# A mixture of experts behind a decoder: rooms of the small experts cut from 128 slots down to 90

## The chip, the core and the metric
The kernel runs on one core of a Trainium2 chip, as one program. The metric is the device time of one execution in microseconds. The kernel before took 1332.15 us, the median of three runs between 1330.96 and 1334.1 us.

## The reference, cut to what matters
```python
x = x + attn(layernorm(x), ...)                 # a state-space scan, 16 x 256 x 256
x = x + align(ctx_1024, layernorm(x))           # dynamic time warping against the context
x = x + ffn(layernorm(x), gate, w0, w1, wo)     # 64 experts, each token goes to 2 of them

# ffn, x is now 4096 tokens x 256
gate_logits = x @ gate                          # 4096 x 64
weights, selected = top_k(gate_logits, 2)
weights = softmax(weights)
# tokens sorted by expert, group_sizes[e] of them for expert e:
h0 = ragged_dot(sorted_x, w0, group_sizes)      # w0, w1: 64 x 256 x 512
h1 = ragged_dot(sorted_x, w1, group_sizes)
out_sorted = ragged_dot(silu(h0) * h1, wo, group_sizes)   # wo: 64 x 512 x 256
out = sum over the 2 experts of weights * unsorted(out_sorted)
```
All of it is float32. The 8192 places (4096 tokens, two experts each) fall on 64 experts, 128 each in the mean. How many each expert gets is known only on the chip.

## The kernel before, in words
The program has five stages, one after the other: `states` (the scan and the distances), `wave` and `trace_back` (the alignment), `expand` (the aligned rows are added, tokens are normalised, routed and listed by expert) and `experts`. The change touches only constants that `expand` and `experts` are built from.

**Rooms.** The experts are ranked by the number of their tokens, most first. The rank fixes how many slots an expert's turn has, its room. `ROOMS` (L47) is a list of entries (first rank, number of ranks, ranks per step, first width, step), and `ROOM` (L48) spreads it out to 64 widths. Ranks 0 to 31 are wide (129 to 256 slots, two tiles of tokens), ranks 32 to 63 narrow (128 at most, one tile). Before, the wide rooms fall from 220 to 134 and the narrow ones are all 128. An expert with more tokens than its room gets late turns for the rest. `LATE` (L56) is the largest possible number of them, and `K.late_n`, which the chip computes, the true number plus one: the last rank, 63, has no turn of its own but always takes the first late turn.

**Order of turns.** `TURN` (L152) alternates: rank 0, 32, 1, 33, ... 31. So 63 turns k are written out, wide for even k and narrow for odd k, and then comes a loop over late turns that runs `late_n` times.

**One turn** (TensorE, L2309 to L2328). With n = room:
- `turn` (L2259, record L2265) transposes the gathered tokens of the next turn into `mo_xt_ps`.
- `up` (L2272, L2279), for each of four blocks m of 128 of the 512 hidden units: four float32 matmuls, stationary operand a 128x128 block of `w0` or `w1`, moving operand n columns of tokens. The profile has two records for one float32 matmul, so 32 records a turn.
- ScalarE makes SiLU of one half of `mo_h` (L2361), VectorE multiplies by the other half (L2408) into `mo_inter`.
- narrow turns: `down` (L2283, L2285), stationary `mo_inter` of n columns, moving 256 columns of `wo`, 8 records. Wide turns: `down_wide` (L2288, L2293), stationary `wo`, moving n columns, 16 records; ScalarE copies the result (L2371) and `back` (L2298, L2304) transposes it inside the next turn.
- VectorE copies the result to `mo_o` (L2419).

The order on TensorE is up 0, up 1, (back of the turn before, if that was wide), up 2, down 0, up 3, down 1, turn of the next, down 2, down 3.

**Queues.** GpSimd gathers tokens four turns ahead by indirect DMA (`gather`, L2213, one for each tile of up to 128 rows) and scatters results (`scatter`, L2220), in the order gather(k+4), scatter(k). Only n rows are moved. SyncE loads the 1.5 MB of weights of turn k once turn k-4 has done its down matmuls (`load_weights`, L2119; ring of four). After the last turn SyncE reads all results back, and VectorE adds them to x with their weights (L2482).

**Constants.** In `expand`, GpSimd writes the rooms into `ro_room` with one IOTA for each entry of `ROOMS` (L1662), then about thirty other constants, between the masks of batch 1 and those of batch 2 (L1645), which TensorE needs for the sums of that batch (L2029). The gate's logits are the matmul at L2050: stationary 128x128 tokens, moving 64 columns of the gate. Tables of late turns (`ro_place`, `ro_at`, `late_of`, `late_at`) have `LATE` or `LATE + 2` columns.

Of the kernel before, what the change touches and what calls it, by code (L numbers as in the profile page):

```python
# [43 lines left out]
WRING = 4  # L44
RANKS = E - 1
WIDE = E // 2
ROOMS = ((0, 2, 1, 220, 20), (2, 14, 2, 190, 6), (16, 16, 2, 148, 2), (32, 32, 32, 128, 0))  # L47
ROOM = [top - step * (i // run) for _, n, run, top, step in ROOMS for i in range(n)]  # L48


# [1472 lines left out]
def expand(K):  # L1523
# [5 lines left out]
    with ExitStack() as c:  # L1529
# [89 lines left out]
        tile = lambda t: K.x[:, t, :]  # L1619
        ALL = 31 + len(ROOMS) + 1  # L1620
        real = lambda b: 0 <= b < B
# [14 lines left out]
        def _(pool):  # L1636
# [23 lines left out]
            def routing_constants():  # L1660
                for r, n, run_, first, step in ROOMS:
                    nc.gpsimd.iota(room[:, r:r + n].rearrange("p (i a) -> p i a", a=run_),  # L1662
# [6 lines left out]
                               ).then_inc(constant, 1)  # L1669
                pool.wait_ge(constant, len(ROOMS) + 4)  # L1670
                nc.gpsimd.affine_select(out=before[:, :], in_=before[:, :], compare_op=ALU.is_gt, fill=0.0,
# [921 lines left out]
```

## Time and profile before
| | us |
|---|---|
| median of three runs | 1332.15 |
| the profiled execution | 1334.92 |
| its span, first to last instruction | 1333.2 |
| TensorE busy | 1051.0 (79%) |
| VectorE busy | 922.2 (69%) |
| ScalarE busy | 577.5 (43%) |
| GpSimd busy | 637.2 (48%) |
| `mo_h` matmuls, 2048 records | 284.2, 290 ns mean |
| SiLU, 256 ACTIVATEs | 71.6, 290 ns mean |

The granted clock of TensorE is 0.886 in the mean. The experts' loop lies between about 835 and 1296 us of the span. A record's duration in this table is its latency; matmuls overlap, so what one costs in a stream is the distance between starts. There are 256 SiLUs, four for each of 64 turns: 63 written out and one late turn.

### The profile page before, as it was taken

Reading aid. Unit: us, or ns where it says so; the run is one execution under the profiler, and the core shown is the slowest. Engines: PE = TensorE matmul, PEld = TensorE weight load, DVE = VectorE, ACT = ScalarE, POOL = GpSimd, SP = SyncE. Lnnn points to the kernel's source line nnn. Section 1 sums busy time; section 2 is a strip of 40 time slices with the busy share of each in tenths; the row PEclk is TensorE's granted clock in tenths of the full one; section 3 lists DMA queues with packets and bytes.
Section 4 is the critical chain, followed back from the end, with each engine's and each line's share of the span. In section 5 each row is a group of like instructions: output and inputs, shape, how many; then the busy total and the mean of one; then the engine's idle time right before and its main releaser. Section 6 shows DMA issues by size and latency. Waiting matters only on the chain. (4 is left out here: it accounts for less than half of the span.)

```text
span 1333.2 us, 21073 instructions
## 1 busy us (share of the span) xinstructions
PE 1051.0 (79%) x6867; PEld 931.6 (70%) x6867; DVE 922.2 (69%) x2071; ACT 577.5 (43%) x1286; POOL 637.2 (48%) x609
## 2 busy tenths in 40 slices
PE   5767878787887875777826886999999999989970
PEld 4656767677776765666412775899999888888860
DVE  6999999999999993888786897233332333222348
ACT  3768787877778672443601652212212111111110
POOL 4886978888786960200003552344344443433420
PEclk8899899999999898555767996899999999999985
DMA  8544546464646532022130112888788788877729
GB/s 241 188 141 140 172 139 198 137 192 151 188 160 187 168 105 66 17 48 32 32 125 2 56 49 76 289 270 274 260 269 279 259 270 274 266 262 262 253 94 352
DMA packets 161165, 231.41 MB, mean 174 GB/s; under 512 B 32157, under 2 KB 85773, under 8 KB 160417
## 3 DMA queue, kind: packets, MB, share of 16 engines
q1 hardware_dynamic: 145520, 206.67, 49.2%
q0 software_dynamic: 9200, 18.96, 4.1%
q10 hardware_dynamic: 6336, 4.44, 1.0%
q8 instruction: 55, 0.90, 0.3%
q14 instruction: 54, 0.43, 0.1%
HBM read 203.01 MB, written 22.80 MB: 169 GB/s over the span
## 5 line engine op out<-in xcount | busy, mean ns | idle before, releaser
L1010 PE MATMUL st_y_ps<-ident,st_hc 128*128 128x128 f32 x2048 | 274.8, 292 | 110.8 <-DVE st_hc L529 110.8
L1010 PEld LDWEIGHTS st_y_ps<-ident,st_hc 128*128 128x128 f32 x2048 | 256.8, 204 | 132.9 <-DVE st_hc L529 132.1
L412 POOL TENSOR_TENSOR st_u<-st_dx,codes 128x1024 f32<-128x1024 f32 x127 | 296.4, 2359 | 39.3 <-DVE st_h L521 31.5
L521 DVE TENSOR_TENSOR_SCAN st_h<-st_da,st_u 128x512 f32<-128x512 f32 x256 | 297.6, 1203 | 0.2 <-POOL st_u L412 0.2
L2279 PE MATMUL mo_h<-mo_xt,w 128*128 128x128 f32 (+17 forms) x2048 | 284.2, 290 | 2.0 <-DVE mo_xt L2402 2.0
L2279 PEld LDWEIGHTS mo_h<-mo_xt,w 128*128 128x128 f32 x2048 | 273.7, 194 | 6.7 <-issue 2.7
L2408 DVE TENSOR_TENSOR mo_inter<-mo_silu,mo_h 128x128 f32<-128x128 f32 (+17 forms) x256 | 75.5, 303 | 280.2 <-ACT mo_silu L2361 217.6
L2361 ACT ACTIVATE mo_silu<-mo_h 128x128 f32<-128x128 f32 (+17 forms) x256 | 71.6, 290 | 315.5 <-PE mo_h L2279 224.9
L2220 POOL DMA_INDIRECT outs<-mo_o,choice x95 | 93.7, 986 | 234.8 <-DVE mo_o L2419 221.0
L748 ACT ACTIVATE st_da<-st_delta,st_a_neg 128x510 f32<-128x510 f32 x256 | 172.1, 685 | 58.3 <-DVE st_h L521 53.7
L529 DVE TENSOR_TENSOR st_hc<-st_h,st_cps 128x1024 f32<-128x1024 f32 x128 | 152.5, 1192 | 0.0
L1294 PE MATMUL wv_e<-wv_r,wv_shift 128*128 128x1 f32 x274 | 75.9, 347 | 40.4 <-DVE wv_r L1232 39.5
L2213 POOL DMA_INDIRECT mo_xg<-xn,table x93 | 90.6, 975 | 33.6 <-issue 28.1
L2293 PE MATMUL mo_ot_ps<-mo_inter,wo 128*128 128x190 f32 (+16 forms) x512 | 89.8, 309 | 17.5 <-DVE mo_inter L2408 14.2
L1294 PEld LDWEIGHTS wv_e<-wv_r,wv_shift 128*128 128x128 f32 x274 | 68.5, 312 | 48.1 <-issue 46.1
L755 ACT ACTIVATE st_cps<-codes 128x512 f32<-128x512 f32 x128 | 76.7, 599 | 43.3 <-DVE st_hc L529 42.2
L2293 PEld LDWEIGHTS mo_ot_ps<-mo_inter,wo 128*128 128x128 f32 x512 | 74.3, 192 | 25.3 <-DVE mo_inter L2408 19.8
L1645 POOL TENSOR_SCALAR ex_on<-ex_apart,ex_reach 128x256 f32<-128x256 f32 x32 | 30.4, 961 | 95.0 <-ACT ex_apart L1972 94.9
L2285 PE MATMUL mo_o_ps<-wo,mo_inter 128*128 128x256 f32 x256 | 73.9, 392 | 0.0
L1284 ACT ACTIVATE wv_r<-wv_e,wv_edge_big 128x1 f32<-128x1 f32 x137 | 35.8, 261 | 64.6 <-PE wv_e L1294 64.6
L1232 DVE TENSOR_TENSOR_SCAN wv_r<-wv_m,wv_r,wave 128x64 f32<-128x64 f32 x136 | 47.8, 352 | 4.8
L2419 DVE COPY mo_o<-mo_o_ps 128x256 f32<-128x256 f32 (+16 forms) x95 | 36.8, 415 | 19.7 <-PE mo_o_ps L2285 17.2
(393 smaller groups left out, 1437.5 us busy)
## 6 DMA issues: line engine op xcount, KB each, us to landing
codes<-bc SPq DMA_DIRECT2D x256, 256.0 KB, 3.7
w<-in_L_ffn_w_dram SPq DMA_DIRECT2D x128, 512.0 KB
wo<-in_L_ffn_wo_dram SPq DMA_DIRECT2D x64, 512.0 KB
co_got<-outs SPq DMA_DIRECT2D x16, 512.0 KB, 6.1
wave<-dist SPq DMA_DIRECT2D x16, 274.0 KB
x<-in_x_dram SPq DMA_DIRECT2D x8, 512.0 KB, 9.1
st_cx<-in_ctx_dram SPq DMA_DIRECT2D x8, 512.0 KB, 4.0
dist<-st_dd SPq DMA_DIRECT2D x32, 128.0 KB, 3.4
```

The costliest lines, as they stand in the source:

```text
L412: nc.gpsimd.tensor_tensor(u_sb[k % URING][:, :, :], dx[p % 2][:, :, :], over_chunks(b_sb[k % BRING]), ALU.mult).then_inc(u_ok, 1)
L521: nc.vector.tensor_tensor_scan(h_sb[k % HRING][:, dh, :], da_ps[dh][:, :], u_sb[k % URING][:, dh, :], 0.0, ALU.mult, ALU.add).then_inc(h_o ...
L529: nc.vector.tensor_tensor(hc_sb[k % RING][:, :, :], h_sb[k % HRING][:, :, :], over_chunks(c_ps[k % 2][:, :]), ALU.mult).then_inc(hc_ok, 1)
L748: nc.scalar.activation(by_batch(da_ps[dh][:, :]), by_batch(delta[p % 2][:, dh, :]), ACT.Exp, scale=a_neg[:, dh, n:n + 1]).then_inc(da_ok, 1)
L755: nc.scalar.activation(c_ps[k % 2][:, :], c_sb[k % CRING], ACT.Copy).then_inc(c_ok, 1)
L1010: m = nc.tensor.matmul(y_ps[t // 2][:, t % 2, dh * P:(dh + 1) * P], hc_sb[k % RING][:, dh, t * P:(t + 1) * P], K.ident[:, :], start=False, ...
L1294: nc.tensor.matmul(e_ps[t % 4][:, 0:1], K.shift[:, :], r[:, t + 1, SW:SW + 1], start=True, stop=True).then_inc(e_mm, 1)
L2213: nc.gpsimd.indirect_dma_start(xg[k % XR][0:n, a, :], None, K.xn_dram[:, :], bass.IndirectOffsetOnAxis(ap=K.table[0:n, at:at + 1], axis=0) ...
L2220: nc.gpsimd.indirect_dma_start(K.outs_dram[:, :], bass.IndirectOffsetOnAxis(ap=K.choice[0:n, at:at + 1], axis=0), o_sb[k % XR][0:n, a, :], ...
L2279: ins = nc.tensor.matmul(h_ps[m][:, i, 0:n], K.w[r][i][:, c_, m * P:(m + 1) * P], xt[u][:, c_, 0:n], start=(c_ == 0), stop=(c_ == DC - 1))
L2293: ins = nc.tensor.matmul(ot_ps[:, c_, 0:n], K.w[r][2][:, m, c_ * P:(c_ + 1) * P], inter[m][:, 0:n], start=(m == 0 and c_ == 0), stop=(m == ...
L2408: nc.vector.tensor_tensor(inter[m][:, 0:n], silu[m][:, 0:n], h_ps[m][:, 1, 0:n], ALU.mult).then_inc(inter_ok, 1)
```

## The change
```diff
-ROOMS = ((0, 2, 1, 220, 20), (2, 14, 2, 190, 6), (16, 16, 2, 148, 2), (32, 32, 32, 128, 0))
+ROOMS = ((0, 2, 1, 220, 20), (2, 14, 2, 190, 6), (16, 16, 2, 148, 2), (32, 8, 8, 128, 0), (40, 16, 1, 124, 1),
+         (56, 7, 1, 108, 3), (63, 1, 1, 128, 0))
```
Ranks 32 to 39 keep 128 slots. Ranks 40 to 55 get 124, 123, ... 109, ranks 56 to 62 get 108, 105, ... 90, and rank 63 keeps 128. Every operation whose size is `room[k]` follows in the turns k = 17, 19, ... 61: the moving columns of `up` and `turn`, the stationary columns of `down`, SiLU and product, the rows of gather, scatter and of the copy to `mo_o`. `LATE` becomes 66 instead of 64, and three more IOTA fill `ro_room`. Nothing else changes, neither the order of turns nor a wait.

## Rows read from the trace of the kernel before
**Rows 1.** By stretch: PE, PEld, DVE, ACT, POOL busy, clock, DMA share, GB/s
```profile
860.00:900.00 40.00, 40.00 (x276) 38.47 (x275) 12.96 (x37) 8.00 (x25) 15.97 (x17) 1.00 0.80 267
...
1140.00:1180.00 40.00, 36.46 (x266) 34.08 (x266) 12.15 (x38) 7.03 (x25) 14.49 (x15) 0.96 0.77 258
```
**Rows 2.** Chain of waits, experts' loop: start, us, what
```profile
1053.55 3.14 PE mo_h L2279 x24
...
1061.11 1.78 PE mo_h L2279 x16
```
**Rows 3.** Waits of SyncE's queue: total us, times, longest
```profile
SPq L156 <- PE mo_ot_ps L2293: 145.0, 29, 6.8
```
**Rows 4.** Timeline, a narrow turn on TensorE: start, us, engine, line, operation, shape, count
```profile
1228.13 1.95 PE L2279 MATMUL mo_h<-mo_xt,w 128*128 128x128 f32 x16
1229.91 0.60 PE L2304 MATMUL mo_o_ps<-ident,mo_ot 128*128 128x128 f32 x4
...
1234.50 2.94 PE L2279 MATMUL mo_h<-mo_xt,w 128*128 128x136 f32 x24
```
**Rows 5.** Timeline, wide turns of 184 and of 136 columns
```profile
912.44 3.90 PE L2279 MATMUL mo_h<-mo_xt,w 128*128 128x184 f32 x24
916.18 0.79 PE L2293 MATMUL mo_ot_ps<-mo_inter,wo 128*128 128x184 f32 x4
...
1237.28 0.63 PE L2293 MATMUL mo_ot_ps<-mo_inter,wo 128*128 128x136 f32 x4
...
1240.17 0.46 ACT L2361 ACTIVATE mo_silu<-mo_h 128x136 f32<-128x136 f32 x2 [2.58 <-PE mo_h L2279]
...
1240.84 1.19 PE L2293 MATMUL mo_ot_ps<-mo_inter,wo 128*128 128x136 f32 x8 [1.32 <-DVE mo_inter L2408]
1241.87 1.39 PE L2279 MATMUL mo_h<-mo_xt,w 128*128 128x128 f32 x11
```
**Rows 6.** Timeline, routing stage, a matmul of 64 moving columns
```profile
752.58 1.06 PE L2050 MATMUL ex_l<-gate,ex_xt 128*128 128x64 f32 x8
753.47 1.08 PE L2029 MATMUL ex_e<-codes,ex_on 128*128 128x256 f32 x4
```
**Rows 7.** Timeline, GpSimd's scatters: 8 rows of a second tile, then 128 rows
```profile
1232.98 0.88 POOL L2220 DMA_INDIRECT outs<-mo_o,choice  x1 [0.30 <-issue]
...
1235.47 1.00 POOL L2220 DMA_INDIRECT outs<-mo_o,choice  x1 [0.30 <-DVE mo_o L2419]
```
**Rows 8.** Timeline, constants, the mask behind them, and who waits for it
```profile
725.85 0.59 POOL L1662 IOTA ro_room<- 128x2 f32 x4
...
731.68 1.82 POOL L1645 TENSOR_SCALAR ex_on<-ex_apart,ex_reach 128x256 f32<-128x256 f32 x2
...
733.56 1.13 PE L2029 MATMUL ex_e<-codes,ex_on 128*128 128x256 f32 x4 [1.34 <-POOL ex_on L1645]
```
**Rows 9.** Timeline, openings, scatters and SiLUs of two wide turns that differ
```profile
1038.77 3.30 PE L2279 MATMUL mo_h<-mo_xt,w 128*128 128x154 f32 x24
1039.71 1.00 POOL L2220 DMA_INDIRECT outs<-mo_o,choice  x1 [0.30 <-DVE mo_o L2419]
...
1044.40 0.68 ACT L2361 ACTIVATE mo_silu<-mo_h 128x154 f32<-128x154 f32 x3 [3.96 <-PE mo_h L2279]
...
1047.00 1.95 PE L2279 MATMUL mo_h<-mo_xt,w 128*128 128x128 f32 x16
...
1095.10 3.14 PE L2279 MATMUL mo_h<-mo_xt,w 128*128 128x146 f32 x24
1097.41 0.99 POOL L2220 DMA_INDIRECT outs<-mo_o,choice  x1 [1.63 <-issue]
...
1101.29 1.95 PE L2279 MATMUL mo_h<-mo_xt,w 128*128 128x128 f32 x16
```
**Rows 10.** Timeline, the late turn: its transposes, and the next gather's landing
```profile
1281.48 0.43 PE L2265 MATMUL mo_xt_ps<-ident,mo_xg 128*128 128x128 f32 x2 [0.52 <-issue]
...
1303.05 0.50 POOL L2250 COPY mo_to<-mo_to_next 128x1 int32<-128x1 int32 x1 [5.60 <-DMA mo_xg<-xn,mo_index]
```

## The prediction
> **What bounds the kernel now.** I read the engines' shares stage by stage first. From 860 to 900 us TensorE is busy for all 40 of 40 us, from 1140 to 1180 for 36.5, at a granted clock of 1.00 (2.4 GHz) and 0.96, while the DMA engines are busy 77 to 80% of the time, VectorE 30% and ScalarE 20% or less [rows 1]. This is the loop over the experts, the only stage in which the width of a room is a loop size. The chain of waits for it has TensorE in nearly every link: turns of a wide and of a narrow expert alternate, and 16 records of `mo_h` in 1.78 us open each narrow turn [rows 2]. SyncE, which fetches the weights, waits 145.0 us for the wide turns alone to free a buffer [rows 3]: weights are not late on average. So what TensorE does in a narrow turn sets the price of a narrower room, and nothing hides a gain there: one narrow turn runs from 1228.13 to 1234.50, 6.37 us, and its records have no idle before them [rows 4].
>
> **The change, part by part.** By the new list ranks 40 to 55 lose 4, 5, ... 19 slots (184 together), ranks 56 to 62 lose 20, 23, ... 38 (203): 387 slots in 23 narrow turns, 16.8 each. The last expert keeps 128.
>
> (a) *The up matmuls*, 32 records a turn, move n columns past 128x128 weights. A record's price is the distance between starts: at 128 columns 16 records in 1229.91 - 1228.13 = 1.78 us, 111.3 ns each [rows 4]. At 184 columns 24 records take 916.18 - 912.44 = 3.74 us, 155.8 ns; at 136 columns 1237.28 - 1234.50 = 2.78 us, 115.8 ns [rows 4, 5]. That is 0.833 ns per column, and carried on it would give 109.2 ns at 128; the measured 111.3 is already above the line. The deciding row is the gate matmul of the routing stage, of the same type and with a 128x128 stationary operand too, but with 64 columns: 8 records from 752.58 to 753.47, again 111.3 ns [rows 6]. Half the columns, the same pace. Every record has a load of 128 columns of weights in front, whatever the room, and I take that as what sets the pace below about 130 columns. Bounds: nothing (the 64-column row), or the column rate carried down, 387 columns x 32 records x 0.833 ns = 10.3 us; a loss has no ground, since fewer columns can't take TensorE longer. The widths in question, 90 to 124, lie between 64 and 128, where both ends cost the same, so I take 0.
>
> The Trainium skill gives two readings of this, both in TensorE: Matmul & The Clock Gate. Its section on the back-to-back issue gap has a formula linear in the moving columns; its section on LDWEIGHTS charges a load by its columns alone, some 107 ns for 128. By the first the edit would gain about 10 us, by the second nothing. The 64-column row agrees with the second.
>
> (b) *The down matmuls* of a narrow expert hold the activations as stationary operand, now of n columns, and move 256 columns of `wo`. At 0.833 ns per column those 256 take 213 ns a record, more than a load, and they stay. Only the first load at a joint could show: if loads shrink with their columns, 16.8/128 x 111.3 = 15 ns, at three joints a turn 23 x 3 x 15 = 1.0 us at most, 0 at least. I take 0, because TensorE has no idle at those joints now [rows 4].
>
> (c) *Turning the tokens in* (two records in the wide turn ahead) moves n columns past 128 columns of stationary operand: same floor as (a), 0. *SiLU and product*: two SiLUs of 136 columns take 0.46 us [rows 5]; even if each shrank by 13%, 0.03 us, TensorE's stream hides it in narrow turns: 0. With that cover gone it would be 4 x 0.03 x 23 = 2.8 us.
>
> (d) *Gather and scatter* carry 387 rows less each way. GpSimd issues a scatter of 128 rows in 1.00 us and that of the 8 rows of a second tile in 0.88 [rows 7]: 1 ns per row, 0.02 us per issue, on an engine that is busy 16 of 40 us [rows 1]. The bytes, 0.8 MB at about 260 GB/s, are 3 us of DMA time spread over 300 us in which DMA is 80% busy [rows 1]. Directly 0, at most 3 us; what a shift of phase does is a rival.
>
> (e) *Setting up.* The list of rooms has 7 entries instead of 4, so GpSimd issues three more IOTA into `ro_room`. Four take 0.59 us, 0.15 each. GpSimd goes from these constants to the mask of the third batch with no idle, and TensorE waits 1.34 us for that mask [rows 8]. So +0.4 us stands on the path; 0 is the lower end, if later beats, in which GpSimd waits for ScalarE, take it back. `LATE` grows from 64 to 66, which lengthens a handful of small VectorE operations by two columns: 0.
>
> (f) *Overflow.* An expert with more tokens than its room gets a late turn more. I worked the counts out of the reference's own inputs. Sorted they are 206, 188, ..., and from rank 40 on 114 (room 124), ..., 96 (99), 95 (96), 91 (93), 74 (90), 51 (128). None is over, so the loop of late turns still runs once, but the closest margin is one token.
>
> **The sum**: 0 (a) + 0 (b to d) + 0.4 (e) + 0 (f) = +0.4 us, which takes the profiled execution from 1334.92 to 1335.3 us. That execution lies 2.8 us above the median of the runs, 1332.15, so I forecast **1332.5 us**, with a range of its own from 1329.6 to 1334.8. A change under 0.2%, 2.7 us, can't be told from none in this kernel.
>
> **The rivals.**
>
> *Late SiLUs in wide turns, for the better.* The 50 records of a wide turn of 136 columns should take some 5.9 us at 0.116 each; the turn takes 1241.87 - 1234.50 = 7.37 us [rows 4, 5]. ScalarE is late in it: its third and fourth SiLU start at 1240.17, although the 24 records that hold the third group of up matmuls end by 1237.44, and then TensorE idles 1.32 us for the product [rows 5]. I can't name what holds ScalarE; DMA issues by SyncE and GpSimd fall in the same stretch. In one turn of 146 columns GpSimd's scatter came 1097.41 - 1095.10 = 2.3 us after the opening and not 1.0, and the turn took 1101.29 - 1095.10 = 6.19 us [rows 9]. If fewer rows relieve whatever it is, a cured turn gives 1.3 us: five give 6.5 us, all 23 give 30. Against it: the rooms shorten an issue by 0.02 us only. Near 1326 us, chance 0.18.
>
> *The same, for the worse (slower than before).* The place is GpSimd's scatter of the narrow tile, in the wide turn behind it. It now starts 0.97 us after the opening (1235.47 against 1234.50) [rows 4, 7]. In an earlier turn it started after 0.94 us (1039.71 against 1038.77), three of four SiLUs came only at 1044.40, and the turn took 1047.00 - 1038.77 = 8.23 us, where the next one of equal width took 1061.11 - 1053.55 = 7.56 by the chain [rows 2, 9]. A shorter gather in front pulls the scatter forward by 0.02 us, to just there. Each turn that tips costs 0.67 us; five decide, since they make 3 us, and 23 would cost 15. Against it: it is one example. About 1337 us, chance 0.15.
>
> *The columns do pay.* The floor in (a) is not there and the up matmuls follow the column rate: 1332.5 - 10.3 = 1322.2 us. For it speaks the straight line through 184 and 136 columns, against it the 64-column row. Chance 0.06.
>
> *It doesn't do what it says.* If the chip's routing differs from my counts by a token or two, the smaller room overflows and adds a late turn. The present one lasts from its transposes at 1281.48 to the landing of the next gather, 1303.05, 21.6 us [rows 10]: 1354 us for one. Chance 0.03.
>
> **How the numbers follow.** The forecast has 0.58, the rivals 0.18, 0.15, 0.06 and 0.03. Faster is 0.18 + 0.06 = 0.24, slower 0.15 + 0.03 = 0.18, within 0.2% 0.58. The range leaves out the column rate, the overflow and the far ends of both SiLU cases, about 2 in 10 with the tails: 1325 to 1338 us.
>
> **What would show it.** Right: openings of narrow turns still take 1.78 us for 16 records, at 90 columns too, and narrow turns stay at 6.37 us; seven IOTA in `ro_room` and TensorE's wait for the third mask some 0.4 us longer; 256 SiLUs as before. Wrong: openings that shrink with the room (16 records of 90 columns near 1.27 us by the column rate); wide turns away from 7.4 us on either side; more than 256 SiLUs; a granted clock clearly under that of before in the second half of the loop.

## The result and the profile after

The changed kernel takes 1322.82 us (median of four runs, 1321.91 to 1323.03) against 1333.12 us (1330.96 to 1335.77) for the kernel before beside it: a ratio of 0.9928, 95% interval 0.9913 to 0.9942. That is 10.3 us or 0.7% faster, 9.7 us below the forecast of 1332.5 us and outside its range. The profiled executions are 1334.92 and 1322.75 us, 12.2 apart. About 2 of these are a single wide turn of the execution before, which took 9.47 us where its neighbours of the same width took 7.46.

From the page of the changed kernel: GpSimd's DMA queue (packets, MB, share of 16 engines) and the groups of the up matmuls, the scatters and the gathers.

```profile
q0 software_dynamic: 13456, 18.23, 4.3%
...
L2280 PE MATMUL mo_h<-mo_xt,w 128*128 128x128 f32 (+40 forms) x2048 | 279.8, 288 | 2.0 <-DVE mo_xt L2403 2.0
...
L2221 POOL DMA_INDIRECT outs<-mo_o,choice x95 | 100.1, 1054 | 208.9 <-DVE mo_o L2420 185.5
...
L2214 POOL DMA_INDIRECT mo_xg<-xn,table x93 | 97.5, 1049 | 33.7 <-issue 28.1
```

The up matmuls, the place where the rooms are a loop size, went from 284.2 to 279.8 us of busy time, and as will be seen that is nearly all overlap. Scatters and gathers, which carry fewer rows now, became longer: their means were 986 and 975 ns before and are 1054 and 1049 ns. The queue has 13,456 packets for 18.23 MB, where it had 9,200 for 18.96 MB.

I cut the span at two events: the first up matmul of turn 0, and the transposes that open the late turn. Before they stand at 836.89 us and 1281.48 [rows 10], after at 839.02 and 1270.98. So the written-out turns take 432.0 us and not 444.6, which is 12.6 less; the start is 2.1 later, and what follows the loop 1.7 shorter (50.0 against 51.7). Read link by link in the chain of waits, the 12.6 are 10.6 from the 23 wide turns of ranks 8 to 30, 1.5 from all narrow turns, and the rest from the first wide ones. Of the 10.6, five wide turns described below give 6.3, the turn of 9.47 us gives 1.9, and the others together 2.4. **The change is made to narrow turns, and the gain lies in wide ones.**

**Narrow turns.** Timeline of TensorE, the last narrow turn, room 90:

```profile
1257.38 1.92 PE L2280 MATMUL mo_h<-mo_xt,w 128*128 128x90 f32 x16
1259.14 0.60 PE L2305 MATMUL mo_o_ps<-ident,mo_ot 128*128 128x128 f32 x4
...
1263.62 2.56 PE L2280 MATMUL mo_h<-mo_xt,w 128*128 128x134 f32 x21
```

The opening of 16 records lasts 1259.14 - 1257.38 = 1.76 us, where 128 columns took 1.78 [rows 4]; the column rate asked for 1.27. The turn takes 6.24 us and not 6.37.

**Wide turns.** Two wide turns of nearly one width. First the turn that opens at 1171.16, with the scatter of a tile of 109 rows (the DVE copy `mo_o` shows the rows):

```profile
1171.16 3.02 PE L2280 MATMUL mo_h<-mo_xt,w 128*128 128x140 f32 x24
1171.37 0.42 DVE L2420 COPY mo_o<-mo_o_ps 109x256 f32<-109x256 f32 x1 [0.60 <-issue]
1172.14 2.34 POOL L2221 DMA_INDIRECT outs<-mo_o,choice  x1 [0.30 <-DVE mo_o L2420]
1172.32 0.29 ACT L2362 ACTIVATE mo_silu<-mo_h 128x140 f32<-128x140 f32 x1 [2.61 <-PE mo_h L2280]
...
1174.06 0.47 ACT L2362 ACTIVATE mo_silu<-mo_h 128x140 f32<-128x140 f32 x2 [1.46 <-PE mo_h L2280]
...
1174.79 0.99 POOL L2214 DMA_INDIRECT mo_xg<-xn,table  x1 [0.31 <-issue]
...
1175.65 0.29 ACT L2362 ACTIVATE mo_silu<-mo_h 128x140 f32<-128x140 f32 x1 [1.13 <-issue]
...
1177.09 1.93 PE L2280 MATMUL mo_h<-mo_xt,w 128*128 128x108 f32 x16
```

Then the one that opens at 1157.36, with a tile of 110 rows:

```profile
1157.36 3.06 PE L2280 MATMUL mo_h<-mo_xt,w 128*128 128x142 f32 x24
1157.56 0.42 DVE L2420 COPY mo_o<-mo_o_ps 110x256 f32<-110x256 f32 x1 [0.59 <-PE mo_o_ps L2286]
1158.37 1.01 POOL L2221 DMA_INDIRECT outs<-mo_o,choice  x1 [0.30 <-issue]
...
1159.69 0.99 POOL L2214 DMA_INDIRECT mo_xg<-xn,table  x1 [0.30 <-issue]
...
...
1161.62 0.29 ACT L2362 ACTIVATE mo_silu<-mo_h 128x142 f32<-128x142 f32 x1 [2.81 <-PE mo_h L2280]
...
1163.11 0.47 ACT L2362 ACTIVATE mo_silu<-mo_h 128x142 f32<-128x142 f32 x2 [1.19 <-PE mo_h L2280]
...
1163.79 1.23 PE L2294 MATMUL mo_ot_ps<-mo_inter,wo 128*128 128x142 f32 x8 [0.54 <-DVE mo_inter L2409]
...
1164.86 1.37 PE L2280 MATMUL mo_h<-mo_xt,w 128*128 128x109 f32 x11
```

The first takes 1177.09 - 1171.16 = 5.93 us, its last SiLU starts 4.5 us after the opening, and no wait is written at its matmuls. The second takes 7.50 us as turns did before, the last two SiLUs start 5.75 us after the opening and right behind that, and TensorE idles. What differs on GpSimd is one number: the scatter of 109 rows holds it for 2.34 us, that of 110 rows for 1.01, so the gathers of the wide tile start 3.63 us after the opening and not 2.33. The 23 wide turns are of these two kinds and some between. One turn each of 144, 142 and 140 columns takes 6.09, 6.01 and 5.93 us, one of 154 takes 6.49 and one of 160 6.74, where all took 7.4 to 7.6 before. These five are turns with a long issue: the tile of 113 rows has its scatter in the first of them, that of 109 rows its gather in the second (2.36 us) and its scatter in the third, the tile of 118 rows its scatter (1.67 us) in that of 154 columns and its gather (1.68 us) in that of 160. A turn of 146 columns takes 6.17 us, but one of that width took 6.19 before too [rows 9]. The other turns from 146 columns down keep 7.1 to 7.5, one takes 8.15, and the last, of 134 columns, takes 5.67 where it took 5.70.

**Setting up.** Timeline of the constants of `expand`:

```profile
725.72 1.03 POOL L1663 IOTA ro_room<- 128x2 f32 x7
...
733.87 1.19 PE L2030 MATMUL ex_e<-codes,ex_on 128*128 128x256 f32 x4 [2.47 <-POOL ex_on L1646]
```

### The profile page after: what moved, and what is told of

It is laid out like the page before. It is cut to its first block and busy times, and to the rows that moved or that the text cites. A ratio compares the mean times of both kernels' runs of the same rounds, so it can differ in the third digit from the quotient of the medians.

```text
span 1321.0 us, 21076 instructions
## 1 busy us (share of the span) xinstructions
PE 1039.5 (79%) x6867; PEld 921.1 (70%) x6867; DVE 921.6 (70%) x2071; ACT 577.0 (44%) x1286; POOL 650.8 (49%) x612
## 3 DMA queue, kind: packets, MB, share of 16 engines
q0 software_dynamic: 13456, 18.23, 4.3%
## 5 line engine op out<-in xcount | busy, mean ns | idle before, releaser
L2280 PE MATMUL mo_h<-mo_xt,w 128*128 128x128 f32 (+40 forms) x2048 | 279.8, 288 | 2.0 <-DVE mo_xt L2403 2.0
L2280 PEld LDWEIGHTS mo_h<-mo_xt,w 128*128 128x128 f32 x2048 | 270.2, 192 | 7.3 <-issue 2.7
L2409 DVE TENSOR_TENSOR mo_inter<-mo_silu,mo_h 128x128 f32<-128x128 f32 (+35 forms) x256 | 74.9, 297 | 267.7 <-ACT mo_silu L2362 213.1
L2362 ACT ACTIVATE mo_silu<-mo_h 128x128 f32<-128x128 f32 (+35 forms) x256 | 71.5, 286 | 303.9 <-PE mo_h L2280 209.8
L2221 POOL DMA_INDIRECT outs<-mo_o,choice x95 | 100.1, 1054 | 208.9 <-DVE mo_o L2420 185.5
L749 ACT ACTIVATE st_da<-st_delta,st_a_neg 128x510 f32<-128x510 f32 x256 | 172.1, 685 | 58.4 <-DVE st_h L522 54.0
L2214 POOL DMA_INDIRECT mo_xg<-xn,table x93 | 97.5, 1049 | 33.7 <-issue 28.1
L2294 PEld LDWEIGHTS mo_ot_ps<-mo_inter,wo 128*128 128x128 f32 x512 | 73.6, 190 | 16.3 <-DVE mo_inter L2409 12.2
L2286 PE MATMUL mo_o_ps<-wo,mo_inter 128*128 128x256 f32 (+23 forms) x256 | 74.1, 392 | 0.9 <-DVE mo_inter L2409 0.9
```

The costliest lines, as they stand in the source:

```text
L749: nc.scalar.activation(by_batch(da_ps[dh][:, :]), by_batch(delta[p % 2][:, dh, :]), ACT.Exp, scale=a_neg[:, dh, n:n + 1]).then_inc(da_ok, 1)
L2214: nc.gpsimd.indirect_dma_start(xg[k % XR][0:n, a, :], None, K.xn_dram[:, :], bass.IndirectOffsetOnAxis(ap=K.table[0:n, at:at + 1], axis=0) ...
L2221: nc.gpsimd.indirect_dma_start(K.outs_dram[:, :], bass.IndirectOffsetOnAxis(ap=K.choice[0:n, at:at + 1], axis=0), o_sb[k % XR][0:n, a, :], ...
L2280: ins = nc.tensor.matmul(h_ps[m][:, i, 0:n], K.w[r][i][:, c_, m * P:(m + 1) * P], xt[u][:, c_, 0:n], start=(c_ == 0), stop=(c_ == DC - 1))
L2286: nc.tensor.matmul(o_ps[k % 2 if isinstance(k, int) else RANKS % 2][0:n, 0, :], inter[m][:, 0:n], K.w[r][2][:, m, :], start=(m == 0), stop ...
L2294: ins = nc.tensor.matmul(ot_ps[:, c_, 0:n], K.w[r][2][:, m, c_ * P:(c_ + 1) * P], inter[m][:, 0:n], start=(m == 0 and c_ == 0), stop=(m == ...
```

## The experiments

They ran in three groups, each beside its own runs of the kernel before (medians 1346.33, 1331.69 and 1331.57 us). The first of these is 1.1% above the others, so each kernel is compared inside its group. All are edits of the kernel before unless said.

### 1. Which half of the change: rows or columns

`e1_rows_only` moves the rows of the changed kernel and computes on the old rooms:

```diff
+MOVES = (... (32, 8, 8, 128, 0), (40, 16, 1, 124, 1), (56, 7, 1, 108, 3), (63, 1, 1, 128, 0))
+rows = lambda k: [(a, at, min(n, MOVED[TURN[k]] - a * P)) for a, at, n in tiles_of(k)]
-                for a, at, n in tiles(k):
+                for a, at, n in rows(k):
```

> The rooms of before (128 columns in every narrow turn), but the gathers and scatters of the 23 narrow experts carry only as many rows as in the changed kernel (124 ... 90). Theory A (row counts): the 10 us come from GpSimd, whose indirect DMAs last 1.0 us for 128 rows but 1.3 to 2.4 us for 123, 122, 118, 113, 109 rows and so on, and so push GpSimd's later issues in a wide turn out of the stretch in which SyncE issues weights; then this kernel is 8 to 12 us faster than before, 1321 to 1325 us, with narrow turns at 6.37 us and wide turns between 5.9 and 7.5 us. Rival B (columns): the matmuls, SiLUs and products of fewer columns bring the time; then it is within 2 us of before.

`e2_columns_only` is the changed kernel, but its narrow gathers and scatters carry 128 rows:

```diff
+rows = lambda k: tiles_of(k) if TURN[k] < WIDE else [(a, at, P) for a, at, _ in tiles_of(k)]
```

> The rooms of the changed kernel for everything computed, but gathers and scatters of narrow experts carry 128 rows again (the surplus goes to dump rows). Theory A: the gain goes; 1331 to 1333 us, wide turns at 7.4 to 7.5 us again, narrow turns 6.24 to 6.37 us, which is 1 to 2 us in all. Rival B: it stays at 1322 to 1324 us.

`e3_rooms_of_16` has rooms that are multiples of 16, with 336 slots less:

```diff
-ROOMS = (... (32, 32, 32, 128, 0))
+ROOMS = (... (32, 14, 14, 128, 0), (46, 13, 13, 112, 0), (59, 4, 4, 96, 0), (63, 1, 1, 128, 0))
```

> Rooms that are multiples of 16: ranks 32 to 45 have 128, 46 to 58 have 112, 59 to 62 have 96; 336 slots fewer than before where the changed kernel has 387 fewer. Theory A: an indirect DMA of 112 or 96 rows lasts 0.94 to 1.0 us, so GpSimd's issues don't move; 1330.5 to 1333.5 us. Rival B (columns or bytes): 336/387 of the gain, some 1324 us.

The times expected were for a kernel before of 1332 us, and this group lies 14 us higher. Measured in it: rows alone 1329.55 us, ratio 0.9875 (0.9849 to 0.99); columns alone 1346.4, 1.0002 (0.9987 to 1.0018); rooms of 16 1344.68, 0.9991 (0.9977 to 1.0005). The whole gain is in the rows of the DMAs; beside its own kernel before `e1` gains 16.8 us, more than the 8 to 12 expected. The third says that it is not the number of rows either: 336 fewer bring nothing, 387 fewer bring 1.2%. Which counts do? Rows of the changed kernel's timeline, copies of a result tile and the scatters of that tile:

```profile
998.18 0.42 DVE L2420 COPY mo_o<-mo_o_ps 122x256 f32<-122x256 f32 x1 [0.55 <-PE mo_o_ps L2286]
999.16 1.68 POOL L2221 DMA_INDIRECT outs<-mo_o,choice  x1 [0.31 <-issue]
```

```profile
1118.36 0.42 DVE L2420 COPY mo_o<-mo_o_ps 113x256 f32<-113x256 f32 x1 [0.59 <-PE mo_o_ps L2286]
...
1119.52 2.38 POOL L2221 DMA_INDIRECT outs<-mo_o,choice  x1 [0.30 <-issue]
...
1130.77 0.42 DVE L2420 COPY mo_o<-mo_o_ps 112x256 f32<-112x256 f32 x1 [0.59 <-PE mo_o_ps L2286]
1131.57 0.96 POOL L2221 DMA_INDIRECT outs<-mo_o,choice  x1 [0.30 <-issue]
```

113 rows take 2.38 us, 112 take 0.96, 122 take 1.68. The other counts fall in place by the largest divisor up to 16. No such divisor but 1 (109, 113): 2.34 and 2.38 us. 2 (118, 122): 1.67, 1.68. 3 (93, 111, 123): 1.33 to 1.42. 4 (116, 124): 1.29, 1.35. 5 to 7 (115, 114, 102, 119): 1.10 to 1.17. From 11 on (99, 110, 121, 108, 117, 90, 105, 120, 96, 112 and 128): 0.94 to 1.04. With s the rows for each share, it is about 0.88 + 0.0133 s us, from 128 rows in 16 shares (s = 8, 1.00) to 113 in one (2.38); an estimate from these rows, and 61 rows in a share give 1.69 by it, measured 1.68.

The Trainium skill has the rule behind this pattern, in DMA: Bandwidth & Descriptors, section "Why a DMA increments its semaphore by 16 and not by 1": a transfer is spread over k engines, k being the largest number up to 16 that divides its slowest dimension. This trace agrees: the durations follow that divisor without an exception in the 23 new row counts, and in the second tiles of wide experts too. On which DMA engines the packets ran the profile does not show.

The kernel before has such issues already. The second tile of a room of 190 has 62 rows (divisor 2), and its scatter is no shorter than one of 128 rows but longer:

```profile
882.41 1.30 POOL L2220 DMA_INDIRECT outs<-mo_o,choice  x1 [0.31 <-issue]
```

The 38 rows of a room of 166 take 1.13 us there, the 72 of a room of 200 only 0.97.

`e1` also has the turns that the changed kernel has short (by its chain 6.10 us at 1121.33, 6.02 at 1148.37, 5.94 at 1174.71). In `e2` and `e3` every turn of 144 to 140 columns takes 7.5 to 8.9 us.

### 2. Take the lateness away directly

`e4_scatter_later`: rooms of before, and GpSimd holds the scatter of the narrow tile back until the second up group of the wide turn is done.

```diff
                 pool.wait_ge(o_ok, k + 1)
+                if not wide[k]:
+                    pool.wait_ge(up_mm, (k + 1) * FC + 2)
```

> The kernel before with one wait more: GpSimd scatters a narrow expert only after the second group of up matmuls of the wide turn behind it, which puts that scatter some 2.0 us behind the opening instead of 0.97, and the two gathers behind it at 3.3 and 4.6 us. No DMA changes. Theory A: all wide turns become like the one of 146 columns that took 6.19 us, 1.0 to 1.4 us less in each of some 28 turns, fewer in the widest: 1298 to 1312 us. Rival C (the long DMA itself matters, not when it is issued): within 3 us of before.

Measured: 1306.1 us, ratio 0.9701 (0.9685 to 0.9717). In a later group the same kernel again:

> e4_scatter_later once more, on the same chip as the next one: 1305.5 to 1307 us. The changed kernel with the same wait (e5) should have been 1.2 us faster by its narrow turns and was not on another chip; this is the mark for the next.

1306.1 us, 0.9807 (0.9794 to 0.9821). The time is the same to 0.1 us, while that of the kernel before differs by 15 us between the two groups, so what varies there is something that the wait removes. Timeline of a wide turn of 142 columns in `e4`:

```profile
1148.14 3.06 PE L2281 MATMUL mo_h<-mo_xt,w 128*128 128x142 f32 x24
...
1149.31 0.29 ACT L2363 ACTIVATE mo_silu<-mo_h 128x142 f32<-128x142 f32 x1 [2.62 <-issue]
...
1150.28 0.29 ACT L2363 ACTIVATE mo_silu<-mo_h 128x142 f32<-128x142 f32 x1 [0.68 <-PE mo_h L2281]
...
1151.01 1.00 POOL L2222 DMA_INDIRECT outs<-mo_o,choice  x1 [2.18 <-PE mo_h L2281]
...
1151.24 0.29 ACT L2363 ACTIVATE mo_silu<-mo_h 128x142 f32<-128x142 f32 x1 [0.68 <-PE mo_h L2281]
...
1152.69 0.29 ACT L2363 ACTIVATE mo_silu<-mo_h 128x142 f32<-128x142 f32 x1 [1.16 <-PE mo_h L2281]
...
1154.17 1.95 PE L2281 MATMUL mo_h<-mo_xt,w 128*128 128x128 f32 x16
```

The scatter starts 2.87 us after the opening. SiLUs come 1.17, 2.14, 3.10 and 4.55 us after it, and the turn takes 6.03 us. All wide turns now go by their columns, 7.70 us at 184 and 5.78 at 136; those of ranks 8 to 30 sum to 144.9 us against 172.1 before and 161.5 after the change. The change had taken 10.6 of these 27.2 us, by accident.

`e6_scatter_after_up1` has the wait with `+ 1`: the pause is one group shorter.

> The kernel before, but the scatter of a narrow expert waits only for the first group of up matmuls of the wide turn behind it: it starts 1.3 to 1.4 us behind the opening instead of 0.97, the two gathers at 2.6 and 3.9. In the changed kernel turns in which the scatter started at 1.30 took 7.1 us and those at 0.97 7.46, those at 2.3 to 2.4 6.0 to 6.2. If the time of issue is all there is to it, this lies between before and e4_scatter_later: wide turns near 7.1 us, 8 to 14 us faster than before.

Measured: 1309.34 us, 0.9836 (0.982 to 0.9852), which is 22 us faster and not 8 to 14. Scatters start 1.9 us after the opening and not 1.3 to 1.4: in `e4` too GpSimd starts its DMA some 0.75 us after the signal of the group that it waits for. In the shorter wide turns the last SiLU is up to 0.3 us later than in `e4`, and one turn of 146 columns takes 7.64 us.

### 3. Who holds the SiLUs back

`e7_weights_later`: SyncE's weight loads in wide turns start only after the last up group, out of the way of the SiLUs in question.

```diff
                 sp.wait_ge(down_mm, (k - WRING + 1) * FC)
+                if wide[k - WRING + 1]:
+                    sp.wait_ge(up_mm, (k - WRING + 1) * FC + FC)
```

> The kernel before, GpSimd untouched, but in wide turns SyncE issues the next weights only after the fourth group of up matmuls, some 4.4 us behind the opening instead of 1.3. Theory A in its full form (GpSimd's and SyncE's DMA issues get in each other's way, and ScalarE's waits with them): moving either engine cures it; 25 to 40 us faster than before, SiLUs prompt (the second near 2.1 us behind the opening), provided the weights still arrive in time. Rival D (GpSimd's indirect DMAs alone hold ScalarE up, whoever issues weights): no gain, SiLUs late as before.

`e8_no_weights`: no weights are loaded for the turns from 4 on, and TensorE waits for the four loads that are left alone.

```diff
                 sp.wait_ge(down_mm, (k - WRING + 1) * FC)
-                load_weights(K, sp, expert_at(K, sp, k), k % WRING)
+                expert_at(K, sp, k)
```

> Leaves out the loads of weights from turn 4 on (but for the late turn), so the experts compute with the weights of the first four. GpSimd issues as before, scatter at 0.97 us. Theory A: all SiLUs prompt, wide turns at the pace of the columns (5.8 us at 136, 7.7 us at 184). Rival D: wide turns stay at 7.4 us.

Measured: `e7` 1330.49 us, 0.999 (0.9981 to 1.0). `e8` 1326.85 us in one run. Of the 22 wide turns of ranks 8 to 29, the second SiLU starts over 4 us after the opening in 13 in the kernel before, in 2 in `e7` and in none in `e8`, mostly 2.8 us instead. But the third starts over 4.9 us after it in 21, 19 and 19 of them, and the third decides. The window from 1140 to 1180 us of `e8` (busy us and count of PE, PEld, DVE, ACT, POOL, then granted clock, DMA share, GB/s), and a wide turn of it:

```profile
1140.00:1180.00 40.00, 37.83 (x293) 35.24 (x291) 12.32 (x39) 7.91 (x27) 17.31 (x18) 1.00 0.13 42
```

```profile
1146.34 3.06 PE L2279 MATMUL mo_h<-mo_xt,w 128*128 128x142 f32 x24
...
1147.29 0.99 POOL L2220 DMA_INDIRECT outs<-mo_o,choice  x1 [0.30 <-DVE mo_o L2419]
...
1149.11 0.29 ACT L2361 ACTIVATE mo_silu<-mo_h 128x142 f32<-128x142 f32 x1 [1.32 <-PE mo_h L2279]
...
1151.28 0.29 ACT L2361 ACTIVATE mo_silu<-mo_h 128x142 f32<-128x142 f32 x1 [1.89 <-PE mo_h L2279]
...
1151.96 1.60 PE L2293 MATMUL mo_ot_ps<-mo_inter,wo 128*128 128x142 f32 x8 [0.42 <-issue]
```

The DMA engines are busy 13% of the time, where the kernel before has 77 to 80% [rows 1], and still the second and third SiLU start 2.77 and 4.94 us after the opening and TensorE idles. SyncE's issues and the traffic of the weights make the second SiLU later, but the idle stays without them; what is left in that stretch is GpSimd.

The traces also tell which engine is late. The chain of waits of the kernel before, in the turn that opens at 1234.50:

```profile
1237.90 2.24 PE mo_h L2279 x8
1240.15 0.02 issue
1240.17 0.29 ACT mo_silu L2361
```

TensorE's signal for the group (the update of the semaphore that ScalarE waits for) comes at 1240.15, and ScalarE starts 0.02 us later. So it is in all 49 SiLUs of the wide turns from rank 4 on that start over 0.3 us late in the kernel before, and in all 38 of the changed one: the update stands 0.02 us ahead of the start. ScalarE is prompt, and **what is late is TensorE's signal**. The signals come in a bunch: in this turn those of up 2, down 0, up 3, down 1 and of the transposes are recorded 5.65, 5.71, 5.80, 5.86 and 5.90 us after the opening. In the short turn of 146 columns of before [rows 9] they come at 3.16, 3.65, 4.65, 5.14 and 5.36 us. Between the first and the last of these signals lie 18 records, 2.1 us at 0.116 us each, and TensorE cannot have done them in 0.25. So its signals were held back, and its matmuls were not.

### 4. A single DMA at a bad moment, or a long run of them

Before, GpSimd issues six indirect DMAs in a row around the opening of a wide turn: two scatters and a gather ahead of it, then the scatter at 0.97 us and gathers at 2.3 and 3.6. Two kernels break the row elsewhere. `e9_wide_gathers_later` leaves the scatter where it is and delays the two gathers behind it:

```diff
                     pool.wait_ge(turned, k - XR + 1)
+                    if wide[k]:
+                        pool.wait_ge(up_mm, (k - XR) * FC + 3)
```

> The kernel before, scatter of the narrow expert at 0.97 us behind the opening as before; only the two gathers for a wide expert wait, for the third group of up matmuls (due at about 2.9 us), so GpSimd's run of six indirect DMAs without a pause (from 2.85 us before the opening to 4.4 behind it) is cut after the fourth. Theory E (a long unbroken run of indirect DMAs makes ScalarE's or TensorE's progress late from about the fourth on): second SiLU somewhat late at most, third and fourth prompt, wide turns 5.8 to 6.3 us at 136 columns, 25 to 40 us faster than before. Theory F (what does it is an indirect DMA issued in the first 2.3 us of a wide turn): second SiLU at 2.8, turns near 7 us, under 15 us faster.

`e10_narrow_gather_later` breaks it one DMA earlier, ahead of the narrow tile's gather, with the scatter and the two gathers right behind:

```diff
+                    if not wide[k]:
+                        pool.wait_ge(up_mm, (k - XR + 1) * FC + 1)
```

> The kernel before, but the gather of a narrow expert waits for the first group of up matmuls of the wide turn; it starts near 1.9 us instead of -0.33, the scatter at 3.2, the wide gathers at 4.5 and 5.8, and the next narrow turn's two scatters follow close. Theory E: the run is now four or more from 1.9 us on, so lateness shows at its end, in the narrow turn (its first SiLUs later than 1.1 and 2.0 us behind its opening); Theory F: wide turns prompt and narrow turns too, as fast as e4, 1306 us.

Measured: `e9` 1306.04 us, 0.9805 (0.979 to 0.982). `e10` 1311.6 us, 0.9848 (0.9833 to 0.9863). A wide turn of 142 columns in `e9`:

```profile
1149.42 3.06 PE L2281 MATMUL mo_h<-mo_xt,w 128*128 128x142 f32 x24
...
1150.40 1.00 POOL L2222 DMA_INDIRECT outs<-mo_o,choice  x1 [0.31 <-DVE mo_o L2421]
...
1152.22 0.59 ACT L2363 ACTIVATE mo_silu<-mo_h 128x142 f32<-128x142 f32 x2 [1.34 <-PE mo_h L2281]
...
1153.26 0.98 POOL L2215 DMA_INDIRECT mo_xg<-xn,table  x1 [1.85 <-PE mo_h L2281]
...
1153.97 0.29 ACT L2363 ACTIVATE mo_silu<-mo_h 128x142 f32<-128x142 f32 x1 [1.16 <-PE mo_h L2281]
...
1155.44 1.95 PE L2281 MATMUL mo_h<-mo_xt,w 128*128 128x128 f32 x16
```

The scatter starts at 0.98 us as before. The second SiLU is late all the same (2.80 and not 2.14), but the third follows right behind it (the x2 at 1152.22), the fourth comes at 4.55 and TensorE is not held up: 6.02 us. So the scatter alone costs one SiLU that has slack, and the idle comes from the gathers behind it. In `e10` the four DMAs run from 1.92 us after the opening into the next, narrow turn:

```profile
1150.80 3.06 PE L2281 MATMUL mo_h<-mo_xt,w 128*128 128x142 f32 x24
...
1152.72 1.01 POOL L2215 DMA_INDIRECT mo_xg<-xn,table  x1 [2.62 <-PE mo_h L2281]
...
1156.62 0.89 POOL L2215 DMA_INDIRECT mo_xg<-xn,table  x1 [0.31 <-issue]
...
1156.84 2.02 PE L2281 MATMUL mo_h<-mo_xt,w 128*128 128x128 f32 x16
...
1163.59 2.67 PE L2281 MATMUL mo_h<-mo_xt,w 128*128 128x140 f32 x21
```

Its wide turn is short (1156.84 - 1150.80 = 6.04 us), but the narrow turn behind it takes 1163.59 - 1156.84 = 6.75 us, where 6.37 is usual [rows 4]. This happens behind wide turns of 148 columns and fewer, but for one of 146 in which GpSimd pauses by itself and the last, in which it gathers nothing. Behind those of 160 and 154 only the first SiLU of the narrow turn is late, 1.3 to 1.6 us after the opening and not 1.09, which costs nothing; the wider the turn, the more of the row of DMAs lies inside it. The lateness moves with the row of DMAs and not with one place in the turn.

### 5. What the columns are worth when nothing else is late

`e5_changed_and_later` is the changed kernel with the wait of `e4`, `e12_rooms16_later` has the rooms of `e3` with it.

> The changed kernel (narrower rooms) with the wait of e4_scatter_later: a candidate for the fastest. If the narrow columns are worth what the narrow turns show (6.24 to 6.37 us against 6.37, some 1.2 us in all) and the row counts cost nothing once GpSimd is out of the way: 0 to 2 us faster than e4's 1306.1, ratio to before 0.967 to 0.971 on a chip like that one. If the long indirect DMAs (2.4 us for 113 or 109 rows) still get in someone's way: slower than e4.

> Rooms of 128, 112 and 96 with the wait of e4: what narrower columns are worth with GpSimd out of the way and with short indirect DMAs. By narrow turns of 6.33 us at 112 columns and 6.27 at 96 against 6.37: 13 x 0.04 + 4 x 0.10 = 0.9 us faster than e11; if the floor of 128 loaded columns holds entirely, no difference.

Measured: `e5` 1306.14 us, 0.9808 (0.9794 to 0.9821); `e12` 1306.2, 0.9802 (0.9789 to 0.9816); `e4` and `e11` 1306.1. No difference that can be measured, where a small gain was expected. The profiles have both halves of it. From the first up matmul to the late turn's transposes the profiled executions need 416.4 us in `e4`, 415.8 in `e11`, 414.4 in `e5` and 414.8 in `e12`: some 1.5 us less, of which the narrow turns give 1.0 to 1.3. But the loops of `e5` and `e12` start at 839.22 and 839.51 us, those of `e4` and `e11` at 837.01 and 836.65, 2.5 us earlier. That is the part on the constants, below.

## Why the prediction was wrong

**The step that failed is (d), gather and scatter.** It priced an issue by its rows, "1 ns per row, 0.02 us per issue", from 128 rows in 1.00 us and 8 rows in 0.88 [rows 7]. Of the 16 new counts from 109 to 124 none divides by 16 but 112. In place of -0.02 us an issue changed by -0.06 to +1.38 us, and in place of "directly 0" the 23 wide turns became 10.6 us shorter, 6.3 of it in the five turns with a long issue. Those two rows could not have shown it. The trace of before could: its scatter of 62 rows takes 1.30 us.

**A rival had the right mechanism and the wrong trigger.** "Late SiLUs in wide turns, for the better" gave 1.3 us a cured turn, and the five cured turns give 0.9 to 1.5 against themselves before. It said against itself that the rooms shorten an issue by 0.02 us only. They lengthen some by 1.4 us, and a long issue works as a pause: it pushes the gathers behind the SiLU that decides. The turn of before that I had quoted, whose scatter came late and which took 6.19 us [rows 9], is the case that `e4` makes the rule; it is no chance, since the same turn has the late scatter in `e1`, `e2`, `e7`, `e8` and `e9` too. All indirect DMAs around it, and not the one scatter, show the row of six. The rival also put the lateness down to ScalarE, and its 50 records at 0.116 us make 5.8 us and not 5.9; without the lateness `e4` has 5.78.

**The rival for the worse** named one turn of 8.23 us. The changed kernel has one, 8.15 us at 1130.57, where the kernel before has two, of 8.23 and 9.47; `e2` and `e3` have several, in a group in which the kernel before was 14 us slower too. The mechanism exists, and no run ties it to a gather that is shorter by 0.02 us.

**(a) The up matmuls** were right: 1.76 us for 16 records at 90 columns, `e2` at 1.0002, and so the rival in which the columns pay is out. Its 1322.2 us is the number nearest to the measured 1322.82, by coincidence. In TensorE: Matmul & The Clock Gate, section "LDWEIGHTS (loading the stationary operand)", the Trainium skill charges a load by its columns, some 107 ns for 128. These rows agree from 128 down to 90 moving columns, at 111 and 110 ns a record. The "about 10 us" that the prediction gave by the other section, on the issue gap, is the slope of this case's rows. By its own formula, N/2.4 ns for N columns, that section of the Trainium skill would give 5.2 us, an estimate, and it says itself that the formula has no share for the load of weights. The floor isn't perfectly flat: I took 0 for (a) and (b), and all narrow turns together lost 1.5 us (0.3 of it in one narrow turn behind that of 9.47), more than the 1.0 us allowed for (b) alone and less than the bounds of the two.

**(e) Setting up** was right in its instructions and too small in effect. Seven IOTA take 1.03 us where four took 0.59, +0.44. From the first IOTA to the matmul behind the third mask it is 733.87 - 725.72 = 8.15 us, and was 7.71 [rows 8]: the +0.4 us of the forecast. (The wait of that matmul, 2.47 us in place of 1.34, was a poor sign to name: it lies between 1.1 and 4.0 us in profiles with four IOTA too.) But the loop starts 2.1 us later. The further 1.7 us are a step that depends on how the engines fall in: from that mask to the next gate matmul with a wait it is 4.0 us in the kernel before and 5.7 in the changed one, and never anything between. With seven IOTA it was 5.7 in four of five profiles, with four IOTA in three of nine. So the setting up costs 0.4 us, and another 1.7 where that step falls so; what decides it I didn't follow.

**(f) Overflow.** No late turn was added: 256 SiLUs as before. In the prediction I gave the counts from rank 40 on as 114; the reference's list begins 116, 115, 114, all below their rooms, and the closest margin is 95 of 96 as stated.

**What stays open.** How GpSimd's row of DMAs holds TensorE's signals back. A single issue of 2.34 us harms less than two of 1.0, and in 19 of the 22 wide turns of before the third SiLU starts 2.1 to 2.3 us after the start of the last gather. Both fit a cause that goes with the number and the start of the DMAs and not with GpSimd's busy time, but that is argued from these turns, and no run tests it. Nor did I follow the 1.7 us that the stretch behind the loop became shorter.

## What to carry to other kernels

When a change touches the row count of a DMA, list the new counts with their largest divisor up to 16 before pricing anything, and keep tiles at multiples of 16 unless measured otherwise. When an engine off the critical path issues a row of DMAs, look at where that row falls in the turns that are longer than their columns explain, and try one wait that breaks it: here one line in the kernel before (1306.1 us) brought two and a half times what the change did, and with it the change itself is worth nothing. A gain that shows up in turns that were not edited is a sign of a shifted phase, and what shifts by accident can be had on purpose.

## What was unexpected about the hardware

- The time to issue an indirect DMA depends on how the row count divides: 0.95 us at 112, 1.00 at 128, 1.68 at 122, 2.38 at 113 rows of 1 KB, and packets of that queue rise from 9,200 to 13,456 with fewer bytes.
- While GpSimd issues four to six indirect DMAs back to back, TensorE's semaphore signals come up to 3.5 us late and in a bunch (five within 0.25 us, 5.65 to 5.90 us after an opening), in a kernel whose DMA engines are busy 13% of the time (`e8`) as in one at 80%. ScalarE starts 0.02 us after the signal. A pause in the row of 1.2 us (`e6`) removes nearly all of it, one of 1.9 or 2.2 us (`e9`, `e4`) removes the idle.
- The kernel before, without the pause, differs by 15 us between groups of runs (1346.33 and 1331.57 us), with it by none (1306.1 and 1306.1).
